# One block for the first layer's plain and distance attention on one Trainium2 core

## The reference

```
scores = einsum('bhid,bhjd->bhij', qh, kh) / sqrt(DH)
p = softmax(where(mask, scores, -1e32)) * mask
cum, tot = cumsum(p), sum(p)
dist = sqrt(clip((tot - cum) * |j - i|, 0))
effect = clip(exp(dist * -softplus(gammas) * exp(sigmoid(pdiff))), 1e-5, 1e5)
scores = softmax(where(mask, scores * effect, -1e32));  scores[:, :, 0, :] = 0
out = einsum('bhij,bhjd->bhid', scores, vh) @ Wo + bo
```

## Time and profile before

| | us |
|---|---|
| median of 3 runs | 1331.24 (1329.02 to 1333.81) |
| the profiled execution | 1336.64 |
| its span | 1334.8 |
| busy DVE | 971.2 (73%) |
| busy PE | 902.6 (68%) |
| busy ACT | 636.2 (48%) |
| busy POOL | 241.3 (18%) |

### The profile page before, as it was taken

One profiled execution on the slowest core, in us unless ns is written; L12 is line 12 of the kernel. 1 busy time (PEld: TensorE's weight loads), 2 busy tenths in 40 slices (PEclk: granted clock), 3 DMA queues, 4 the chain that ended last, 5 costly groups with the idle time before them and its releaser, 6 DMA issues. The chain is left out here.

```text
span 1334.8 us, 18469 instructions
## 1 busy us (share of the span) xinstructions
PE 902.6 (68%) x6150; PEld 590.7 (44%) x6150; DVE 971.2 (73%) x2494; ACT 636.2 (48%) x1392; POOL 241.3 (18%) x370
## 2 busy tenths in 40 slices
PE   5964666745788402345797957898978626998876
PEld 3532233332455202234695633576645304566644
DVE  5859898956666399987455856798868497898822
ACT  4746777750444412353413731787437411666632
POOL 1320000001000000000012211189522022232100
PEclk9975555556899755676898987899979766999968
DMA  5000000001254300110100000000000000000000
GB/s 208 1 1 0 0 1 0 0 0 61 79 124 102 88 0 22 45 65 33 32 2 1 2 1 1 0 1 1 1 1 1 1 0 0 1 2 2 1 1 16
DMA packets 26607, 30.12 MB, mean 23 GB/s; under 512 B 1169, under 2 KB 23057, under 8 KB 25490
## 3 DMA queue, kind: packets, MB, share of 16 engines
q1 hardware_dynamic: 26514, 28.95, 7.7%
HBM read 19.50 MB, written 9.44 MB: 22 GB/s over the span
## 5 line engine op out<-in xcount | busy, mean ns | idle before, releaser
L1771 PEld LDWEIGHTS l2a_b_ps<-l2a_diag,l2a_uT 128*128 128x128 f32 x512 | 64.7, 194 | 29.1 <-issue 16.6
L1771 PE MATMUL l2a_b_ps<-l2a_diag,l2a_uT 128*128 128x128 f32 x512 | 69.2, 279 | 6.4 <-DVE l2a_convh L1982 5.4
L2468 PE MATMUL l1w_mem_ps<-l1a_rows,l1w_post 128*128 128x64 f32 x16 | 4.7, 391 | 95.7 <-DVE l1a_rows L2610 95.7
L2583 DVE MATCH_REPLACE8 l1w_minus<-l1w_low,l1w_minus 128x129 f32<-128x129 f32 (+39 forms) x264 | 64.4, 256 | 0.0
L2496 ACT ACTIVATE l1w_score<-l1w_mix_ps 128x264 f32<-128x264 f32 (+7 forms) x29 | 12.0, 451 | 108.9 <-DVE l1a_rows L2610 92.4
L2577 DVE MAX8 l1w_low<-l1w_minus 128x8 f32<-128x129 f32 (+37 forms) x332 | 59.5, 254 | 0.4
L2458 PE MATMUL l1w_mix_ps<-l1a_rows,l1w_pre 128*128 128x264 f32 (+7 forms) x58 | 30.5, 697 | 43.0 <-DMA l1a_rows<-scores_dram 24.8
L2441 POOL TENSOR_SCALAR_AFFINE_SELECT l1w_score<-l1w_score 128x256 f32<-128x256 f32 x8 | 4.1, 507 | 249.0 <-ACT l1w_score L2496 249.0
L2468 PEld LDWEIGHTS l1w_mem_ps<-l1a_rows,l1w_post 128*128 128x128 f32 x16 | 4.3, 306 | 100.7 <-DVE l1a_rows L2610 99.5
L583 ACT ACTIVATE l3a_l3x_probT<-l3a_l3x_turn_ps 128x512 f32<-128x512 f32 x64 | 38.2, 596 | 21.9 <-PE l3a_l3x_turn_ps L479 21.1
L1012 ACT ACTIVATE l0x_prob<-l0x_dist,l0x_last_mx 128x128 f32<-128x128 f32 x128 | 38.2, 386 | 21.5 <-DVE l0x_last_mx L1135 21.5
(11 more groups left out here) (579 smaller groups left out, 2809.9 us busy)
## 6 DMA issues: line engine op xcount, KB each, us to landing
scores_dram<-l1p_dots SPq DMA_DIRECT2D x8, 924.0 KB, 7.1
l1a_rows<-scores_dram SPq DMA_DIRECT2D x5, 1056.0 KB, 4.9
l1a_rows<-scores_dram SPq DMA_DIRECT2D x24, 132.0 KB, 3.6
scores_dram<-l1p_dots SPq DMA_DIRECT2D x8, 132.0 KB, 3.6
pack<-in_pack SPq DMA_DIRECT2D x1, 761.5 KB, 9.6
pack<-in_pack SPq DMA_DIRECT2D x2, 321.5 KB, 6.7
pack<-in_pack SPq DMA_DIRECT2D x1, 612.0 KB, 11.6
pack<-in_pack SPq DMA_DIRECT2D x1, 576.0 KB, 10.5
```

The lines of the kernel that those rows point to most:

```text
L1771: mm = nc.tensor.matmul(bx_ps(n)[:, j * S:(j + 1) * S], uT[:, c, b, :], diag[:, s % 2, b, :], start=True, stop=True)
L2583: nc.vector.match_replace(out=neg[:, i, 0:keys[i]], in_to_replace=low[:, i, :], in_values=neg[:, i, 0:keys[i]], imm_value=LOWEST).then_inc ...
```

## The change

The two blocks become one. `distance_attention` becomes a class `DistanceAttention`, whose methods `pool`, `tensor`, `scalar` and `vector` give each engine's pieces; the plain attention gets the object as `then` and calls the pieces at given steps. The second attention uses the plain attention's PSUM banks (`use`) and has its own SBUF tiles. In detail:

- PE projects q and k of distance batch 0 at now = 5 and of batch 1 at now = 6, and makes both halves of the scores of batch 0 at now = 7, ahead of `transpose_probs(7, 0, 1)`, after waits on the plain differences of batch 7. After now = 9 it waits for all eight xT copies of the plain attention and runs `rest`.
- DVE sets the constants ahead of the plain attention's first copy, copies batch 0's and 1's projections at now = 6 and 7 between statistics and scaling, makes batch 0's differences at now = 7 around the division of batch 6, and batch 0's scans, rates and products (`then_remaining(0)`) at now = 8 between statistics and scaling of batch 6. `rest` begins with `second_scores(0)`.
- ACT makes batch 0's first exponentials at now = 7. The xT copies of plain batches 6 and 7 are moved behind batch 0's root and exponential (`earlier`), then V's copy of batch 0 follows.
- POOL sets the second v pair ahead of its loop. The addition over all of x is gone; each plain store adds the bias instead (`next_bias`).
- The wait of DVE for all eight grids becomes one per batch.

The hunks in `attention`:

```diff
@@ -322,7 +322,7 @@
     prefix: bool = False
 
 
-def attention(nc, cm, layers, project=True, src="x", distances=None):
+def attention(nc, cm, layers, project=True, src="x", distances=None, then=None):
 
     xT = cm.xnT if src == "xn" else cm.xT
     kvT = lambda b: (cm.ctxT if spec(b).kv == "ctx" else xT)[:, b % B, :]
@@ -344,6 +344,8 @@
         v_ps, y_ps, oT_ps, nT_ps = (row_bank[:, n * D:(n + 1) * D] for n in range(4))
         turn_ps = turn_bank[:].rearrange("p (h t) -> p h t", h=HH)
 
+        if then:
+            then.use(qk_bank, sums_bank, row_bank, turn_bank, scores)
         q = [sc.sb(f"q{n}", [128, S]) for n in range(2)]
         km = [sc.sb(f"km{n}", [128, HH, S]) for n in range(2)]
         v = [sc.sb(f"v{n}", [128, H, 32]) for n in range(2)]
@@ -355,6 +357,8 @@
         o = sc.sb("o", [128, D])
         oT = sc.sb("oT", [128, D])
         ln = LayerNorm(sc)
+        if then:
+            then.x_stored = ln.x_stored
         k_flat = sc.sb("k_flat", [128, S])
         k_set, km_set = sc.sem("k_set"), sc.sem("km_set")
         if any_rope:
@@ -404,6 +408,15 @@
                     need(pool)
                     pool.tensor_tensor(cm.x[:], cm.x[:], bcast_mid(w(0, "bo"), B), ALU.add).then_inc(skip_set, 1)
 
+                if then:
+                    cm.need(pool, then.name)
+                    then_rest = then.pool(pool)
+
+                def next_bias(b):
+                    if then:
+                        return then.w("bo")
+                    return w(b + B, "bo") if b + B < T else None
+
                 def spread_keys(b):
 
                     after(pool, scores_mm, 2 * (b - 1))
@@ -418,13 +431,15 @@
 
                 for now in range(-1, T + 2):
                     if inside(now - 2):
-                        ln.pool_store(pool, cm, now - 2, w(now - 2 + B, "bo") if now - 2 + B < T else None)
+                        ln.pool_store(pool, cm, now - 2, next_bias(now - 2))
                     if FIRST <= now + 2 < T and spec(now + 2).rope:
                         spread_keys(now + 2)
                     if FIRST <= now + 3 < T and not spec(now + 3).rope:
                         spread_keys(now + 3)
                     if distances and inside(now - 2):
                         distances.pool_step(pool, now - 2)
+                if then:
+                    then_rest()
 
             @block.tensor
             def _(pe):
@@ -535,6 +550,8 @@
                     pe.wait_ge(v_set, min(b + 3, T))
                     ln.pe_transpose(nc, pe, cm, nT_ps, b)
 
+                if then:
+                    then_project, then_score, then_rest = then.tensor(pe)
                 project_qk(0)
                 for now in range(-1, T + 2):
                     if now < 0:
@@ -545,6 +562,10 @@
                             project_qk(1)
                     if inside(now + 2):
                         score_prefix(now + 2)
+                    if then and now == T - 1:
+                        for half in range(2):
+                            pe.wait_ge(diff_set, 2 * T - 1 + half)
+                            then_score(0, half)
                     if inside(now):
                         transpose_probs(now, 0, 1)
                     if inside(now - 1):
@@ -558,6 +579,12 @@
                         project_v(now + 1)
                     if inside(now + 3):
                         project_qk(now + 3)
+                    if then and now == T - 3:
+                        pe.wait_ge(qk_set, T)
+                        cm.need(pe, then.name)
+                        then_project(0)
+                    if then and now == T - 2:
+                        then_project(1)
                     if inside(now):
                         transpose_probs(now, 1, 1)
                     if inside(now - 1):
@@ -572,6 +599,9 @@
                         project_out(now - 1)
                     if inside(now):
                         weigh(now, 1)
+                if then:
+                    pe.wait_ge(ln.xT_set, T)
+                    then_rest()
 
             @block.scalar
             def _(act):
@@ -628,13 +658,15 @@
 
                 if distances:
                     distances.act_begin(act)
+                if then:
+                    then_first, then_rest = then.scalar(act)
                 for now in range(-1, T + 2):
                     if inside(now):
                         copy_probT(now, 0, 0)
                         exponential(now, 1)
                         exponential_prefix(now)
                         copy_probT(now, 0, 1)
-                    if inside(now - 2):
+                    if inside(now - 2) and not (then and now >= T):
                         ln.act_copy(act, nc, cm, nT_ps, now - 2)
                     if inside(now):
                         copy_prefix(now)
@@ -642,8 +674,12 @@
                     if inside(now + 1):
                         copy_v(now + 1)
                         exponential(now + 1, 0)
+                    if then and now == T - 1:
+                        then_first(0, 0)
                     if inside(now):
                         copy_probT(now, 1, 1)
+                    if then and now == T - 1:
+                        then_first(0, 1)
                     if inside(now - 1):
                         copy_out(now - 1)
                     if FIRST <= now + 3 < T and not spec(now + 3).rope:
@@ -652,6 +688,9 @@
                         distances.act_step(act, now)
                     if inside(now):
                         copy_sums(now)
+                if then:
+                    cm.need(act, then.name)
+                    then_rest(lambda: [ln.act_copy(act, nc, cm, nT_ps, b) for b in (T - 2, T - 1)])
 
             @block.vector
             def _(dve):
@@ -757,16 +796,27 @@
                         dve.wait_ge(skip_set, 1)
                     ln.dve_stats(dve, nc, cm, y_ps if project else o[:], b)
 
+                if then:
+                    then_copy, then_constants, then_differences, then_remaining, then_rest = then.vector(dve)
+                    then_constants()
                 copy_qk(0)
                 for now in range(-1, T + 2):
                     if inside(now - 2):
                         statistics(now - 2)
+                    if then and now == T:
+                        then_remaining(0)
+                    if then and now == T - 2:
+                        cm.need(dve, then.name)
+                    if then and T - 2 <= now < T:
+                        then_copy(now + 2 - T)
                     if inside(now + 2) and now >= 0:
                         copy_qk(now + 2)
                     if inside(now - 2):
                         ln.dve_scale(dve, nc, cm, now - 2)
                     if inside(now + 1):
                         maximum(now + 1, 0)
+                    if then and now == T - 1:
+                        then_differences(0, 0)
                     if now < 0:
                         copy_qk(now + 2)
                         if any_prefix:
@@ -778,8 +828,12 @@
                     if inside(now + 1):
                         maximum(now + 1, 1)
                         prefix_difference(now + 1)
+                    if then and now == T - 1:
+                        then_differences(0, 1)
                     if distances:
                         distances.dve_step(dve, now)
+                if then:
+                    then_rest()
 
 
 class Distances:
```

The class holds the old functions unchanged but for these places (cut):

```diff
+        def project_qk(b):
+            pe.wait_ge(cm.ctx_loaded, 16)
...
+    def scalar(self, act):
...
+        def rest(earlier):
+                if inside(now) and now:
+                    first_weights(now, 0)
...
+                if inside(now) and now:
+                    first_weights(now, 1)
+                    copy_v(now)
+                if inside(now):
+                    load_root_table()
...
+                if now == 0:
+                    earlier()
+                    copy_v(0)
+                if inside(now):
+                    exponential(now, 0)
...
+    def vector(self, dve):
...
+        def remaining(b):
...
+            dve.wait_ge(distances.grid_set, b + 1)
...
+        def statistics(b):
...
+            if b == 0:
+                dve.wait_ge(self.x_stored, B)
...
+        def rest():
...
+                if inside(now) and now:
+                    for half in range(2):
+                        differences(now, half)
+                    remaining(now)
...
+                if inside(now + 1) and now:
+                    copy_qk(now + 1)
```

More of the change, by code:

```diff
@@ new lines, in pool @@
+    def pool(self, pool):
+        nc, cm = self.nc, self.cm
+        v = self.v
+        ln = self.ln
+        zero_set = self.zero_set
+        ones_set = self.ones_set
+        for n in range(2):
+            pool.memset(v[n][:], 0.0).then_inc(zero_set, 1)
+        for n in range(2):
+            pool.wait_ge(zero_set, n + 1)
+            pool.memset(v[n][:, :, DH:DH + 1], 1.0).then_inc(ones_set, 1)
+        def rest():
```

(97 more changed lines are left out.)

585 lines of the change are left out of this document (288 added, 297 removed).

## The result

| | before | after |
|---|---|---|
| median, us | 1332.22 (1329.02 to 1333.81, 4 runs) | 1316.40 (1315.62 to 1318.07, 4 runs) |
| the profiled execution, us | 1336.64 | 1316.28 |
| its span, us | 1334.8 | 1314.5 |

The ratio is 0.9886 with a 95% interval of 0.9869 to 0.9903: 12.9 to 17.5 us less, where 13.1 were forecast. A second set of runs, further down, gave 0.9907 (0.9890 to 0.9923), 10.2 to 14.6 us less.

The account below looks back on a forecast made before the run. VectorE bounds the distance attention but works only 5.7 of 17 us in the valley before it; filling that gives 14.76 - 1.4 - 0.15 - 0.1 = 13.1 us, so the median 1331.24 becomes 1318.1, range 1314.0 to 1323.0.

Parts of the forecast that it names:

- the stretch: VectorE, from the end of the last plain score difference to distance batch 1's second first-maximum; forecast gain 13.1 us.
- the sum to L1126: VectorE's work from the last plain difference to batch 0's L1126: 22.11 us instead of 36.87, so 14.76 earlier.
- the hand-over: Batch 1's scores queue behind late xT copies and V's projection, coming 1.5 us later; cost 1.4, bounds 0 and 1.95.
- the extra instructions ahead: `then_constants` before the plain attention's first projection copy costs 0.15 us, `then_copy(0)` in a wait for the root 0.1.
- rival 2: More than forecast: the hand-over to batch 1 costs nothing, gain 14.5 to 15 us, time 1316.5; chance 0.12.
- The cover: Last plain steps, 3.15 us on VectorE, fit under ScalarE's 3.49 us root, table load and exponential, 0.3 to spare.
- TensorE's scores in the plain tail: Both `then_score` halves before batch 7's transpositions take 1.55 us each; the 1.8 us delay is hidden by 0.3.
- Rival 1, the cold tail: TensorE's clock falls at 76 us, scores take 3.1 us each, gain 9.4; 0.15 together with port rule and between.
- The rule that spoke against it: GpSimd's root for batch 6 is blocked by VectorE's two-operand scans and products; gain 12.5 instead of 13.1 us.
- Rivals 3 and 4: 3: ScalarE's queue prevents overlap, 1327 us, chance 0.04. 4: gaps halve TensorE's plain-attention clock, slower, up to 1343, chance 0.03.
- the signs: L1126 some 22 us after the last plain difference, no VectorE idle over 1 us between, later stages shifted by one constant.

Follow-up runs that it names:

- second set of runs: The changed kernel measured again without an edit: median 1317.39 us, ratio 0.9907 (0.9890 to 0.9923) against the kernel before.
- the kernel before again: The kernel before, traced a second time without an edit: stretch 44.33 us against 44.39, span 1330.1 us against 1334.8.
- the late scan: Changed kernel with batch 0's scans, rates and products moved behind the plain attention's last step: 1321.49 us, stretch 35.20 us.
- Taking the queue apart: Changed kernel with batch 1's scores ahead of V's projection and V copied after batch 1's first exponential: 1315.03 us, ratio 0.9878.
- removing the barrier alone: Changed kernel with one block but all batch 0 pieces behind the plain attention: 1328.3 us, ratio 0.9989 to the kernel before.

## Why the prediction was right

**The time and the stretch.** The stretch became 14.19 us shorter, where 13.11 were forecast, and the missing 1.08 us are in the terms: 0.62 in the sum to L1126, 0.21 in the hand-over, 0.25 for the extra instructions ahead, which cost nothing. All erred to the same side. The median fell by more, 15.8 us, and by 13.4 in the second set; the difference from 14.19 lies within what stages outside the change vary by, as the trace of the kernel before again shows. So where in the range the median fell is in part luck. It is nearest to rival 2's 1316.5, but not for its reason: that rival said that the hand-over costs nothing, and it cost 1.19.

**The sum to L1126.** 22.11 us were forecast from the last plain difference to L1311 (the old L1126), 21.49 were measured in both traces; so it comes 15.38 us earlier instead of 14.76. Each from its start to its end, the terms were nearly as forecast: the copies took 0.98 where 1.01 stood, the differences 2.69 and 2.68 where 5.40 stood for both, division and statistics 0.57 + 0.90 where 1.53 stood, scans to products 9.50 for 9.52, and the ScalarE piece 3.49 for 3.49. Most of the missing 0.62 has one cause: I added such durations, but at the seams between them VectorE begins the next instruction before the end of the one ahead (76.55 + 0.35 = 76.90, next start 76.81). Six seams of that kind, 0.08 or 0.09 us each and 0.51 together, were counted twice. It isn't so at every seam: L170, which reads what L168 has written, starts 0.04 us after its end (74.72 + 0.28 = 75.00, then 75.04).

**The cover.** The 3.15 us of plain steps fitted under ScalarE's 3.49 with 0.29 us of waiting left, as forecast (0.3). Without that cover VectorE waits the whole 3.49, as the late scan shows.

**The hand-over.** 1.4 us were forecast, by scores that come 1.5 late. The rows give 0.73 + 0.28 of waits, and from L1311 to the second maximum 8.71 us where before it was 120.26 - 112.74 = 7.52: 1.19 us. Taking the queue apart gave 1.16 of it back. Right in mechanism, 0.2 too large: the scores start 98.92 - 97.21 = 1.71 us after the end of ScalarE's exponentials, where 1.95 stood, so they come 1.26 late and not 1.5. Part of this is the same double counting: they start 0.21 us before the end of V's projection (98.34 + 0.79 = 99.13). The clock was 0.50 there, as assumed.

**TensorE's scores in the plain tail.** 1.55 us each were taken as half of the cold row. The first group's two parts start at 74.78 and 75.32, the second group's at 76.38: 1.60 a group, at a granted clock of 1.00. VectorE's division of batch 6 started at 79.41 without a wait, so the 0.3 us of cover held. Rival 1, the cold tail, did not occur: the granted clock was 1.00 from 74 to 84 us in every trace.

**The start.** The constants were priced at 0.15 and `then_copy(0)` at 0.1. The constants hold the first copy by 0.19 us, but not the scores behind it, and from the sixth plain difference to the last it takes 36.94 to 36.98 us in all nine traces, with `then_copy(0)` in it or not. So both terms were 0. What was not in the sum is larger: the last plain difference starts between 73.58 and 75.92 us in the traces of the changed kernel and at 74.64 and 75.37 in those of before. All of this arises in the first steps, and the granted clock goes with it. Here are 14 to 30 us of the first trace after, the first of before, and the second after:

```profile
14.00:30.00 16.00, 11.80 (x81) 6.77 (x82) 12.33 (x18) 9.42 (x16) 3.32 (x10) 1.00 0.45 181
14.00:30.00 16.00, 12.60 (x62) 7.22 (x62) 10.38 (x14) 8.40 (x14) 2.01 (x5) 0.89 0.44 179
14.00:30.00 16.00, 12.71 (x56) 6.96 (x56) 10.22 (x17) 7.13 (x11) 3.09 (x9) 0.79 0.45 180
```

In the two traces with 1.00 the last plain difference starts at 73.58 and 73.74, in the five with 0.89 between 74.40 and 75.37, and in the two with 0.79 at 75.91 and 75.92. So the first trace after had a start 1.1 us quicker than the first of before, at the higher clock. None of the runs tells what decides that.

**The rule that spoke against it.** Here the choice was wrong, though nothing hung on it, which was luck. I went by the earlier trace rows, in which a GpSimd product beside a VectorE addition lost 0.05 us, and took it that the two run together. The traces show the exclusion: GpSimd's root took 2.10 and 2.48 us beside the scans, 0.19 and 0.55 without them. This is the rule of the Trainium skill ("SBUF — State Buffer", section "Who interferes with whom"): a VectorE instruction with two SBUF inputs contends with a GpSimd instruction that reads SBUF. By that rule, these traces agree. It goes the other way too: the addition at L168 takes 0.52 us instead of 0.28 where GpSimd's grid product (93.52, 0.45 us) began 0.07 before it:

```profile
93.59 0.52 DVE L168 TENSOR_TENSOR l0a_ln_r<-l0a_o,x_tok 128x128 f32<-128x128 f32 x1
```

My price for the rule, 0.6 us, assumed the root to be held up to the last product. It got through, one instruction beside each scan, and was ready at 88.12, ahead of the products and 4.6 us ahead of its reader. The row that I went by doesn't speak against the exclusion: the VectorE instruction of the earlier trace rows ended at 61.33, so it could hold GpSimd's product, begun at 61.14, for 0.19 us at most, and 0.05 is what the product lost. Why not more, no run shows.

**Rivals 3 and 4, and the signs.** The overlap is there, and the plain attention's clock stayed full (1.00 in 56.00 to 63.00 as in 57.00 to 64.00 of before), so neither happened. VectorE's longest wait up to L1311 was 0.93 us. Batch 1's product with the scores comes 45.82 us after the last plain difference (it starts at 120.63) and came 60.01 after it before (135.88): 14.19 us less, the same as the stretch. Up to the quantized feed-forward's last scaling, counted from the last plain difference, the two traces of before take 249.0 and 249.3 us and those of after 235.0 and 234.4: 14.0 to 14.9 us less, so that the steady batches kept the shift. From there to the end of the span it takes 1009.9 and 1004.2 us before, 1004.7 and 1003.8 after. That the shift stays constant thus holds against the second trace of before. Against the first it doesn't, by the last stage above all, which varied by 3.9 us between executions of one and the same kernel. The medians' 13.4 and 15.8 us are the gain within that noise.

## What to carry to other kernels

An engine that bounds two stages but idles between them is worth a look at the seam: count what it does in the valley, and move the head of the next stage there in the order in which its inputs are ready. Keep small steps of the old stage for the first long wait of the new one; moving them out from under ScalarE's root, table load and exponential cost 5.0 us, while removing the barrier alone was worth 2.2. Then look at what queues behind the moved steps on the other engines, since the hand-over back to the steady order is where part of the gain is lost (1.2 us here).

## What the hardware showed that was not expected

- An instruction of GpSimd that is shut out by VectorE is shown as running, not as waiting: L80 has a duration of 2.10 us for one element a partition. In the kernel with the late scans the same happened to the store of x and the grid product, which took 0.41 and 0.45 us a step earlier in that trace:

```profile
89.01 2.34 POOL L199 TENSOR_TENSOR x_tok<-l0a_ln_xn,pack 128x128 f32<-128x128 f32 x1 [0.46 <-DVE l0a_ln_xn L179]
91.31 2.45 POOL L868 TENSOR_TENSOR l_grid<-l_grid,pack 128x128 f32<-128x128 f32 x1
```

- The scans lost little. With the root waiting beside them they took 4.47 us for the two, 4.50 without. Beside the store and the grid product they took 4.67: the first scan 2.30 us, the second, which started at 91.07 while the store ran until 91.35, 2.45 instead of 2.28.
- The blocked instructions ended close to the end of a scan: L80 at 85.57 and L82 at 88.12, the scans at 85.59 and 87.78; in the late scans L199 at 91.35 and L868 at 93.76, the scans at 91.15 and 93.52. So here the length of VectorE's scan, 2.3 us, set the time of GpSimd's instruction, whether that needs 0.19 or 0.55 us alone.
